# Three first loads change places and queues, and one dummy matmul goes: a fused graph-layer kernel on one NeuronCore

## What is computed

```
h    = x @ W_loop.T                       # [128 nodes, 128]
g    = h @ Wg_loop.T
vals = (h + b_loop) * sigmoid(g + bg_loop)
x1   = layernorm(x + relu(adj.T @ vals))
y    = (adj == 1) @ x1 @ weight[0] + bias
out  = layernorm(x1 + y)
```

## Time and profile before

| | |
|---|---|
| runs | 157.73, 157.86, 158.17 us |
| the profiled execution's own time | 158.45 us |
| its span, first to last instruction | 156.8 us |
| PE, DVE, ACT, POOL busy | 149.6, 137.6, 127.9, 117.0 us |
| TensorE's granted clock, mean | 0.989 |

### The profile page before, as it was taken

One profiled execution on the slowest core, in us unless ns is written; L12 is line 12 of the kernel. 1 busy time (PEld: TensorE's weight loads), 2 busy tenths in 40 slices (PEclk: granted clock), 3 DMA queues, 4 the chain that ended last, 5 costly groups with the idle time before them and its releaser, 6 DMA issues.

```text
span 156.8 us, 3842 instructions
## 1 busy us (share of the span) xinstructions
PE 149.6 (95%) x1055; PEld 139.0 (89%) x1055; DVE 137.6 (88%) x546; ACT 127.9 (82%) x293; POOL 117.0 (75%) x225
## 2 busy tenths in 40 slices
PE   6999999999999999999999999999999999999940
PEld 3589899999999999999999999999999999999940
DVE  1348989599999999999999999999999999999980
ACT  4378897579888888899888888899888888879960
POOL 1426898998777787798777787798777786776870
PEclk9999999999999999999999999999999999999995
DMA  3999999978989999999999989999989853161154
GB/s 119 345 387 377 406 399 396 394 233 267 293 276 293 299 296 314 319 267 304 298 287 309 305 282 307 297 302 313 315 272 303 263 183 134 67 201 71 67 201 144
DMA packets 19607, 42.74 MB, mean 273 GB/s; under 512 B 2176, under 2 KB 2816, under 8 KB 19584
## 3 DMA queue, kind: packets, MB, share of 16 engines
q1 hardware_dynamic: 14400, 25.76, 49.0%
q0 software_dynamic: 4896, 16.52, 33.1%
q10 hardware_dynamic: 288, 0.20, 0.4%
HBM read 34.08 MB, written 8.39 MB: 271 GB/s over the span
## 4 chain that ended last, share of the span: by engine, by line
PE 88%; DVE 5%; issue 2%; POOL 1%; POOLq 0%; DVEq 0%
PE hg_ps L489 35%; PE loop_ps L506 18%; PE y_ps L598 16%; PE msg_ps L574 16%; PE hg_ps L472 1%; PE msg_ps L478 1%; DVE last_stats L1037 1%; POOL last_rstd L422 1%; DVE x L1007 1%; PE aux_ps L574 1%; POOL last_rstd L412 1%; DVE s_sb L981 0%; DVE z_sb L1024 0%; POOLq L281 0%; PE aux_ps L618 0%
## 5 line engine op out<-in xcount | busy, mean ns | idle before, releaser
L489 PE MATMUL hg_ps<-w_all,xt_sb 128*128 128x256 f32 x256 | 61.0, 382 | 0.0
L395 POOL TENSOR_SCALAR x<-s_sb,rstd,nmr 128x128 f32<-128x128 f32 x114 | 49.7, 448 | 3.5 <-PE msg_ps L574 0.3
L489 PEld LDWEIGHTS hg_ps<-w_all,xt_sb 128*128 128x128 f32 x256 | 46.6, 192 | 6.0 <-issue 0.8
L386 POOL TENSOR_TENSOR rstd<-var,power 128x4 f32<-128x4 f32 x31 | 32.0, 1032 | 18.4 <-DVE var L946 16.1
L742 ACT ACTIVATE out_sb<-z_sb,rstd 128x128 f32<-128x128 f32 x100 | 34.1, 391 | 0.2 <-DVE rstd L913 0.2
L695 ACT ACTIVATE hg_ps<-gate_b 128x1024 f32<-128x1024 f32 (+1 forms) x32 | 31.9, 999 | 1.6 <-DVE vals L954 1.1
L506 PE MATMUL loop_ps<-vals,adj_sb 128*128 128x128 f32 x248 | 32.9, 276 | 0.1
L704 ACT ACTIVATE gate<-hg_ps 128x512 f32<-128x512 f32 x32 | 19.0, 594 | 16.9 <-PE hg_ps L489 16.9
L598 PEld LDWEIGHTS y_ps<-w,msg_t 128*128 128x128 f32 x240 | 31.3, 191 | 1.5
L598 PE MATMUL y_ps<-w,msg_t 128*128 128x128 f32 x240 | 31.8, 275 | 0.0
L506 PEld LDWEIGHTS loop_ps<-vals,adj_sb 128*128 128x128 f32 x248 | 30.4, 192 | 0.5 <-issue 0.2
(11 more groups left out here) (100 smaller groups left out, 125.0 us busy)
## 6 DMA issues: line engine op xcount, KB each, us to landing
xt_sb<-x_t_dram SPq DMA_DIRECT2D x32, 256.0 KB, 4.3
x_sb<-x_dram SPq DMA_DIRECT2D x32, 256.0 KB, 4.4
out<-out_sb SPq DMA_DIRECT2D x32, 256.0 KB, 3.3
adjt_sb<-adj_t_dram POOLq DMA_DIRECT2D x15, 512.0 KB, 5.0
adj_sb<-adj_dram POOLq DMA_DIRECT2D x14, 512.0 KB, 5.1
adj_sb<-adj_dram POOLq DMA_DIRECT2D x3, 256.0 KB, 6.9
adjt_sb<-adj_t_dram POOLq DMA_DIRECT2D x2, 256.0 KB, 8.6
raw<-adj_dram SPq DMA_DIRECT2D x1, 256.0 KB, 3.9
```

The lines of the kernel that those rows point to most:

```text
L386: nc.gpsimd.tensor_tensor(r, var1[:, q % 2, :], power[:, :], ALU.pow).then_inc(rstd1_done, 1)
L395: done = nc.gpsimd.tensor_scalar(x1[:, q % X1_RING, batch(b)], s_sb[:, q % S_RING, batch(b)], r[:, b:b + 1], n[:, b:b + 1], ALU.mult, ALU.add)
L489: last = nc.tensor.matmul(hg_ps[:, q % 2, b, :], xt_sb[:, q % XT_RING, batch(b)], w_gate, start=False, stop=True, skip_group_check=True)
```

## The change

Wg_loop.T moves from the first place of SP's queue to the second of ScalarE's. The load of x transposed for group 0 takes the first place on SP, so W_loop.T stays second and everything behind `load_xt(1)` moves up by one issue. The gate's bias leaves ScalarE's queue and becomes the first transfer that GpSimd issues, ahead of its first memset. Of the four dummy matmuls behind the fold three are left.

```diff
@@ block.sync
-            sp.dma_start(wg_t[:, :], wg_loop_t).then_inc(fold_in, 16)
+            load_xt(0)
             sp.dma_start(w_all[:, P:2 * P], w_loop_t).then_inc(w_gate_in, 16)
-            load_xt(0)
             load_xt(1)
@@ block.gpsimd
+            pool.dma_start(gate_b[:, :], gate_bias).then_inc(bias_in, 16)
             nc.gpsimd.memset(power[:, :], -0.5).then_inc(power_ready, 1)
@@ block.tensor
             nc.tensor.matmul(aux_ps[:, 0:P], w_loop, wg_t[:, :], start=True, stop=True).then_inc(fold_done, 1)
-            for _ in range(4):
+            for _ in range(3):
                 nc.tensor.matmul(msg_ps[:, :], warm[:, :], warm_wide, start=True, stop=True)
@@ block.scalar
             act.dma_start(w_all[:, 0:P], w_in).then_inc(fold_in, 16)
-            act.dma_start(gate_b[:, :], gate_bias).then_inc(bias_in, 16)
+            act.dma_start(wg_t[:, :], wg_loop_t).then_inc(fold_in, 16)
```

## The result

The changed kernel takes 160.86 us, the median of 3 runs (160.07 to 162.03), against 157.86 us: a ratio of 1.0172, interval 1.0121 to 1.0223. It is slower by 1.7%, outside the forecast range, and on a side that the prediction gave 0.34. The profiled execution took 162.03 us, with a span of 160.4. It is the slowest of the three, so the traces differ by 3.6 us where the medians differ by 3.0.

What follows compares the result with a forecast made beforehand. TensorE, busy 149.6 of the 156.8 us span, was taken as the bound. Later fold and bias, less one dummy, start the projections 0.26 us later, +0.13 us at half clock: 158.0 us against 157.86, range 157.5 to 159.4.

Steps and rivals of the forecast that it cites:

- The sum: Start of the projections: 5.84 instead of 5.58, 0.26 us later, counted at half clock as +0.13 us.
- What bounds the kernel, and what each start waits for: Whole kernel: TensorE bounds it, busy 149.6 of 156.8 us; only its earlier or later start wins or loses time.
- The fold's operand: Ahead of the fold: wg_t lands at 3.8, between 3.5 and 4.1, so projections cannot start before 5.67.
- The bias: Gate bias on GpSimd's queue, the deciding term: issued at 0.86, lands at 5.0, so the projection starts at 5.84.
- Half price ahead of 6.8: Before the clock reaches 2.4 GHz near 6.8, a microsecond of delay of project(0) costs 0.5 us; afterwards all of it.
- Rival 3: Holes around the fold delay the clock's rise, slowing the first projections by 0 to 2.85 us: 159.4 us, 1.6 in 10.
- rival 2: Bias is a long new wait: landing up to 7.2, products at 8.0, +1.8 us, 159.7 us; 1.6 in 10.
- The dummy and x transposed: Behind the fold: one dummy less removes 0.43 us, about paying for the later fold; earlier x transposed gives at most 0.1.

Runs made afterwards that it cites:

- small_first: The changed kernel with SP's first two loads exchanged, W_loop.T first and x transposed for group 0 second: 160.71 us, ratio 1.0141 to the kernel before.
- xt_second: The kernel before with three dummies behind the fold and x transposed for group 0 second on SP's queue, between the two weights: 158.54 us, ratio 1.0019.
- xt_first_sp: The kernel before with one edit, x transposed for group 0 ahead of both weights on SP's queue: 160.27 us, ratio 1.0125.
- bias_alone: The kernel before with one edit, the gate's bias moved from ScalarE's queue to first transfer on GpSimd's: 158.53 us against 158.09, ratio 1.0024.

## Why the prediction was wrong

The sum had two terms that were mis-sized and one that was missing. The start was to come 0.26 us later and came 2.02 us later, it was to count half and counted whole, and the clock's rise was to stay in place and cost 1.8 us. Behind all three stands the 256 KB load in SP's first place, beside a slip of 0.5 us in the bias's issue.

**What bounds the kernel, and what each start waits for: right.** The fold's rule (fold load + 0.58 + 0.43 for each dummy) and the bias's rule (landing + 0.84) both held: 4.53 + 1.87 = 6.40 for the end of the dummies in the changed kernel, where its row ends at 6.61 with 0.2 us of the last one's tail, and 6.77 + 0.84 = 7.61 for the products, which started at 7.60.

**The fold's operand: the step that failed first.** I bounded the landing of `wg_t` by 3.5 and 4.1, pricing 192 KB more at 318 GB/s. It landed at 4.49, and the fold started at 4.53. The rate came from a full stretch later on; at the start it was 181 GB/s (192 KB at that rate are 1.1 us, which would have given 4.6). That is a mean with the DMA engines idle for half of the time, and no price of a byte. I also held W_loop, whose place does not change, for unaffected. It took 3.3 us. The runs give the price: 1.0 to 1.5 us for whatever small load is issued beside or right behind a 256 KB one at the start (W_loop 3.3 us instead of 2.0, `wg_t` 3.2 and in small_first 3.6 instead of the 2.2 of its like, the bias 3.9 in xt_second instead of 2.4). Why W_loop's packets come late is open.

**The bias: right as the last wait, wrong in the size and in the reason.** The landing was 6.77, not 5.0, inside the bounds (3.3 to 7.2) but near the one that I had moved away from. Half a microsecond is a plain slip: the issue was at 1.40, not at 0.86, since POOL's queue had 0.83 us of idle time before it. I had put it where the first memset of the queue stood. The step from issue to first packet was right (the packets begin at 3.5, 2.1 us behind the issue). The step from first packet to landing was 3.3 us and not 2.05, near its slow value. I had let being the program's first software transfer speak for the slow values. The runs show 3.2 us to landing when that edit is made alone, and 4.5 us on ScalarE's queue with the large load ahead. The cause was the traffic that the first edit had moved ahead and beside it. The Trainium skill's rule ("DMA: Bandwidth & Descriptors", section "Anatomy of one DMA"), an estimate of 2.3 us, is nearer to the quiet cases, 3.2 and 3.5, than to the changed kernel's 5.4.

**Half price ahead of 6.8: wrong.** It took the place of the clock's rise as fixed while the start moved behind it, and the holes moved it as well. Its own rule, with the real start of 7.60, would have given 1.4 us (half of 1.22, and 0.8). The start cost its full 2.0 us, and the rise another 1.8.

**Rival 3, the clock: right, at 1.4 us against 1.8, but held apart from rival 2.** The chances treated them as exclusive. They have one cause: the load that makes the fold and the products late also makes the holes. The hole ahead of the fold was 1.03 us and not the 0.5 of the prediction, which had the dummies' row end at 3.3 where it ends at 3.50. Rival 2 and rival 3 together, by my own prices, would have given 161, and the measurement is 160.9. That they meet so well is partly luck: rival 2 had the start at 8.0, and it was 7.6.

**The dummy and x transposed: right.** One dummy less is worth nothing by itself, and nothing downstream waited for SP's loads or for line 428.

## What to carry to other kernels

In the first microseconds several small transfers gate the first real work, so the size of what is issued ahead of them counts: here 256 KB moved ahead of them, or issued in the same moment on another queue, delayed them by 1.0 to 1.5 us, more than its bytes at the later rate, and 64 KB by 0.2 to 0.3. Ask first what the load gained by its early place (here 0.1 us) and then what everything issued beside it must land for. And where a new wait leaves TensorE idle ahead of the rise of its clock, count the wait and the later rise together, since they come from one cause; dummy matmuls up to the end of the wait take the second part away.

## What the hardware showed that I had not expected

A 64 KB transfer whose place, queue and neighbours on its queue did not change landed 3.2 us behind its issue (W_loop in xt_first_sp) instead of 2.0, because another queue issued 256 KB at the same time. In the changed kernel, where it took 3.3, the DMA engines stood nearly idle for part of that time. A 128 KB transfer had 45 of its 48 packets and all its bytes behind it by 4.4 and landed at 6.77, beside a hardware queue that held 69% of the engines' time from 4.4 to 6.5; without that traffic it landed 1.9 us sooner. The same kernel's runs spread widely at this start: the kernel before, 25 times on one chip, took 157.8 to 159.7 us. The clock's rise is a part of it: bias_alone's sixteen products took 3.56 us where those of the kernel before took 4.07, with the same instructions and no hole in either, and they account for 0.5 of the 0.8 us between the two spans. Whether it is all of it was not tried.
